# Deciding the gate in two halves, and ScalarE scaling the experts' hidden rows, in a decoder kernel

## What is computed

```python
xn = rmsnorm(xf, gate_norm_w, EPS)
gate_logits = bitlinear(xn, gate_in_norm_w, gate_w)
probs = softmax(gate_logits)
topw, topi = top_k(probs, 2)
# one expert:
pos = cumsum(keep0) - 1            # over the tokens in order
keep = keep0 & (pos < C)           # C = 512, the room of an expert
xin = xf[tok] where valid
h = bitlinear(xin, gpn, gpw)
g, y = split(h)
out = bitlinear(silu(g) * y, dpn, dpw)
outputs.at[tok].add(out * wtok)
# bitlinear(x, norm_w, w):
xn = rmsnorm(x, norm_w, 1e-8)
q = round(xn * 127 / max(|xn|)) per row;  weights rounded to -1, 0, 1 times their mean
```

## Time and profile before

| | us |
|---|---|
| median of three runs | 2256.37 |
| lowest, highest | 2253.13, 2257.48 |
| the profiled execution's own time | 2251.49 |
| its span in the trace | 2249.6 |

### The profile page before, as it was taken

One profiled execution on the slowest core, in us unless ns is written; L12 is line 12 of the kernel. 1 busy time (PEld: TensorE's weight loads), 2 busy tenths in 40 slices (PEclk: granted clock), 3 DMA queues, 4 the chain that ended last, 5 costly groups with the idle time before them and its releaser, 6 DMA issues. The chain is left out here.

```text
span 2249.6 us, 43362 instructions
## 1 busy us (share of the span) xinstructions
PE 1692.2 (75%) x13330; PEld 1072.2 (48%) x13330; DVE 1547.2 (69%) x3321; ACT 1448.7 (64%) x2313; POOL 757.3 (34%) x732
## 2 busy tenths in 40 slices
PE   3789899999989999898589886021454478998577
PEld 1455555555555555555367664021122246666323
DVE  6877777777777777776525657662677377876775
ACT  2888889798888989798144656452455344443845
POOL 0534545455454545455000000085000156554000
PEclk9999999999999999999778878555566689999799
DMA  6222222222222222222312110362111311321001
GB/s 189 53 52 65 60 58 65 51 66 54 65 53 61 57 60 57 56 61 48 107 38 75 66 48 1 134 217 69 68 37 38 112 38 38 38 30 26 1 10 66
DMA packets 173816, 139.94 MB, mean 62 GB/s; under 512 B 83794, under 2 KB 155399, under 8 KB 173366
## 3 DMA queue, kind: packets, MB, share of 16 engines
q1 hardware_dynamic: 166710, 122.78, 20.5%
q0 software_dynamic: 6912, 14.71, 3.3%
HBM read 61.92 MB, written 20.97 MB: 37 GB/s over the span
## 5 line engine op out<-in xcount | busy, mean ns | idle before, releaser
L577 ACT ACTIVATE a_p_hi<-ps,a_probs_up,a_s_scale 128x512 f16<-128x512 f32 x512 | 397.7, 777 | 57.6 <-ACTq L575 56.8
L689 DVE TENSOR_REDUCE a_top<-ps 128x2 f32<-128x1024 f32 x256 | 313.3, 1224 | 134.0 <-DVEq L688 133.9
L578 ACT ACTIVATE a_probs<-ps,a_probs_up,a_s_scale 128x512 f32<-128x512 f32 x512 | 398.4, 778 | 0.0
L917 POOL TENSOR_TENSOR a_p_lo<-a_probs,a_p_hi 128x1024 f16<-128x1024 f32 x128 | 278.4, 2175 | 208.9 <-POOLq L916 168.6
L905 POOL TENSOR_TENSOR a_ops<-a_ident_down,a_top 64x256 f16<-64x256 f32 x256 | 158.9, 621 | 344.7 <-POOLq L900 336.2
L698 DVE TENSOR_TENSOR a_p_lo<-a_probs,a_p_hi 128x1024 f16<-128x1024 f32 x128 | 182.6, 1427 | 41.1 <-DVEq L697 41.1
L441 PE MATMUL ps<-a_ops 128*128 128x512 f16 x512 | 196.3, 383 | 17.6 <-PEq L439 17.6
L460 PE MATMUL ps<-a_v_hi,a_p_hi 128*128 128x65 f16 x2048 | 206.2, 197 | 3.2 <-PEq L455 2.9
L463 PE MATMUL ps<-a_v_lo,a_p_hi 128*128 128x64 f16 x2048 | 206.1, 195 | 0.0
L464 PE MATMUL ps<-a_v_hi,a_p_lo 128*128 128x65 f16 x2048 | 206.0, 196 | 0.0
L460 PEld LDWEIGHTS ps<-a_v_hi,a_p_hi 128*128 128x128 f16 x2048 | 191.6, 99 | 23.9 <-issue 11.9
(11 more groups left out here) (495 smaller groups left out, 3723.4 us busy)
## 6 DMA issues: line engine op xcount, KB each, us to landing
a_ops<-a_qk SPq DMA_DIRECT2D x384, 128.0 KB, 2.3
f_w<-in_L_ffn_W_dram SPq DMA_DIRECT2D x16, 1024.0 KB, 7.5
a_qd<-a_qk SPq DMA_DIRECT2D x128, 64.0 KB, 2.2
g_stage<-in_L_attn_gp_w_dram SPq DMA_DIRECT2D x8, 1024.0 KB, 6.6
X<-in_x_dram SPq DMA_DIRECT2D x8, 512.0 KB, 9.6
expert_in<-g_w SPq DMA_DIRECT2D x8, 512.0 KB
g_stage<-in_L_attn_dp_w_dram SPq DMA_DIRECT2D x8, 512.0 KB, 7.6
e_x_in<-expert_in SPq DMA_DIRECT2D x8, 512.0 KB, 4.3
```

Of the source, the lines that this page charges most:

```text
L577: nc.scalar.activation(p_hi[:, h % 2, k, :], scores, ACT.Exp, bias=probs_up[:], scale=s_scale[:])
L578: nc.scalar.activation(probs[:, h % 2, k, :], scores, ACT.Exp, bias=probs_up[:], scale=s_scale[:]).then_inc(st_taken, 1)
L689: nc.vector.tensor_reduce(top[:, c % 2, 2 * pair:2 * pair + 2], ps[:, ROW:ROW + 2, :], AX.X, ALU.max).then_inc(row_taken, 1)
L917: nc.gpsimd.tensor_tensor(p_lo[:, h % 2, 2:KT, :], probs[:, h % 2, 2:KT, :], p_hi[:, h % 2, 2:KT, :], ALU.subtract).then_inc(p_made_pool, 1)
```

## The change

1. The gate's rows run in four stages rather than five (L1050 and the new methods): norms are folded into `gate_roots`, which makes the four inverse roots (one more reciprocal in place of a second chain) in one set of Newton rounds on 128x16. On ScalarE the squares move from `experts_rows` to their own `square`, between `quantise` and `pair_turned(b, 1)`. On TensorE `gates` moves from behind `f_rows` to behind the values. On VectorE `add_outputs` stands ahead of logits, roots and values.
2. The choice moves into `GateRows` and is made for tiles 0 to 15 and 16 to 31 apart, with a carry of counts between them. The first half stands in `middle`: the maximum in step 7, the choice at the start and the slots at the end of VectorE's step 8, the counts on TensorE in step 8; GpSimd sends the first 32 scatters as the last thing of its part of `middle`. The second half stands in the next block, ahead of the weights' staging. The zeros over the inbox are written in `middle`, from a tile (f_outT) that GpSimd clears.
3. In the experts VectorE weighs the rows by the norm weights alone as each tile comes (`weigh`) and takes maxima of these; the inverse root and the quantising factor are multiplied into one number by row (h_per). ScalarE scales by it and adds the rounding constant (`hidden_round`, four operations), then rounds as before. The weighed rows lie in gate_u, which is free by then. ScalarE rounds the next expert's rows ahead of the results.
4. In the masked attention `maximum` is split, and at t = 3 VectorE does `outputs` ahead of the maximum and of `add_x`.

Cut to its core:

```diff
-    NORMS, ROWS, SQUARES, QUANTISE, GATES = 1, 2, 3, 4, 5
+    VALUES, ROOTS, QUANTISE, GATES = 1, 2, 3, 4
+    CHOICE = B // gate.HALVES - 1 + GATES
...
+                gate.masks(pool)
+                nc.gpsimd.memset(outT[:].rearrange("p c s -> p (c s)"), 0.0).then_inc(zeros_made, 1)
...
+                pool.wait_ge(gate.zeroed, 16 * (E + 1))
+                pool.wait_ge(u_made, B // gate.HALVES)
+                gate.send(pool, 0)
...
-                    if 0 <= b - GATES < B:
-                        gates(b - GATES)
                     if b + 1 < B:
                         scores(b + 1, bank_of["scores", b + 1])
...
                         values(b, 1)
+                    if 0 <= b - GATES < B:
+                        gates(b - GATES)
                     if 1 <= b <= B:
                         for m in range(DC):
                             outputs(b - 1, m)
+                    if b == CHOICE + 1:
...
+                        gate.count(pe, bank_of["counts",])
...
+                    if b == CHOICE + 1:
+                        gate.choose(dve, 0)
+                    if b >= B and b - ROOTS < B:
+                        gate_roots(b - ROOTS)
                     if 1 <= b <= B:
                         add_outputs(b - 1)
...
+                    if b == CHOICE:
+                        gate.less_maximum(dve, 0)
...
+                    if b == CHOICE + 1:
+                        gate.slots(dve, 0, bank_of["counts",], free[bank_of["counts",]])
...
+                    gate.less_maximum(dve, HALF)
+                    gate.choose(dve, HALF)
+                    gate.slots(dve, HALF, 2)
...
+                    def hidden_round(j):
+                        act.wait_ge(h_factor, 1)
+                        act.sem_inc(h_factor, -1)
+                        for t in range(RT):
+                            nc.scalar.activation(weighed[:, j, t, :], weighed[:, j, t, :], ACT.Identity, scale=h_per[:, t:t + 1],
+                                                 bias=plus_round[:])
...
                         act.drain().then_inc(h_squared_all, 1)
+                        if not last:
+                            whole(r[:], a[:], a_round, r_made)
                         if not first:
                             results((j + 1) % 2)
...
+                    def weigh(e, j, tiles):
+
+                        dve.drain()
+                        for t in tiles:
+                            nc.vector.tensor_tensor(weighed[:, j, t, :], h[:, t, :], down_n[:, e, :], ALU.mult)
...
-                        for t in range(RT):
-                            nc.vector.scalar_tensor_tensor(out=h[:, j, t, :], in0=h[:, j, t, :], scalar=rstd[:, t:t + 1],
-                                                           in1=down_n[:, e, :], op0=ALU.mult, op1=ALU.mult)
+                        nc.vector.tensor_tensor(h_peak[:], h_peak[:], rstd[:], ALU.mult)
...
+                        if t == 3:
+                            outputs()
+                            if more:
+                                maximum(t)
+                            add_x(b, t - 1)
```

481 lines of the change are left out of this document (270 added, 211 removed).

## The result

| | before | changed |
|---|---|---|
| median, us | 2256.93 | 2228.86 |
| lowest, highest | 2253.13, 2261.93 | 2223.41, 2234.56 |
| profiled execution's own time | 2251.49 | 2223.41 |
| its span | 2249.6 | 2221.7 |

The ratio is 0.9875, with a 95% interval of 0.9842 to 0.9907: 28 us faster, where 22.5 was forecast (2228.9 against 2234). The sum came nearly right, but of its terms one was half of what it turned out to be and one had the wrong sign, and several pieces of the difference between the two traces stand in stretches that the change doesn't touch. Five kernels have a single execution each and are read from their traces alone: the experts' old order, the two with the gate product moved, and the two without the squares.

What follows compares the result with a forecast made beforehand. No engine is full; each touched stage is a ring of waits, bound by the one ending last. -12 (`middle` and gate stage) - 7.5 (experts) - 3 (masked attention) = -22.5, from the 2256.4 median to 2234 us; 80% range 2214 to 2250.

Steps and rivals of the forecast that it cites:

- The two edits that I priced: `middle`: squares leave the place ahead of the probabilities' copy (at most 5.1 us); gate's product behind the values (4.2 and 2.4).
- the product's wait ahead of step 5: `middle`, TensorE: no 3 us wait before the gate's product, step 5 near 31 us, as a sign in the later trace.
- 11.7 gross and 8 net: `middle`: TensorE waits removed, 11.7 us, less 3.6 for the squares' new place in four steps; net 8, bounds 0 and 13.
- rival A: Slower by the clock: `middle`'s steps 3 to 6 at step 5's pace, masked scores perhaps slow; 2273 us, chance 0.08.
- The first scatter: End of `middle`, GpSimd: first scatter starts at 1417.6, after VectorE's first slots at 1425.6 less part 1's 8 us.
- the block was held: `middle`'s end: 32 scatters at 1.28, 41 us, keep the block open to 1458.6; without them it would have ended near 1427.
- Rival B: `middle`'s end: scatters at the contended 1.65, 53 instead of 41 us, all behind 12 later; about 2245, chance 0.2.
- The order of the rounding: Experts, ScalarE: rounding the next rows ahead of the results takes 1.3 us from a period, from two TensorE waits.
- The scaling: Experts, ScalarE: four scalings of 0.75 add 3.0 us a period, while its idle of 2.58 goes.
- The mean of 22.8: Experts: mean period before, taken over seven experts against a forecast ring of 21.7, for -7.5, bounds 0 and -18.
- Rival C: Experts go to VectorE's ring, 19.4 us a period, 14 us more gain; 2220, chance 0.12.
- 0.4 us a batch: Masked attention: gain from taking the outputs earlier, counted for seven batches, -3 us in all, bounds +2 and -8.

Runs made afterwards that it cites:

- the experts' old order: Kernel before with part 3, but the next rows' rounding behind the results again on ScalarE; period mean 22.4 us over the first six.
- the best of these versions: Changed kernel with part 4 undone, 10 of the first 32 scatters left in `middle` and 22 behind the block's end; ratio 0.9796 (0.9768 to 0.9823).

## Why the prediction was right, point by point

**Part 1, `middle`.** Its steps 3 to 7 took 157.26 us before and 141.54 after, 15.7 less, and 8 were forecast with a bound of 13. The two edits that I priced are the two that the runs found (10.7 for the product's place; 3.9 for the squares in their old place, of which 2.4 remain in the new one), and the product's wait ahead of step 5 went as said. The step that failed is the price of a wait on TensorE. I added up idle time, 11.7 gross and 8 net, as if a wait that is taken away were gone and the work beside it stayed as long as it was. Neither held: over steps 3 to 6 TensorE's idle fell only from 20.3 to 16.3 us, since much of it moved to the next product, and its work fell from 110.2 to 98.0, at a higher clock. So 4 of the 16 us in these four steps are idle, and 12 are work that I had left as it was. My rival A was the same mechanism with the other sign, and it had a place in the range of possible losses but none in the gain.

**Part 2, the halves.** The mechanism was right link by link. The first scatter was forecast for 1417.6 and came at 1401.5. Counted from `middle`'s first weights that is 12.1 earlier: 3.6 stand ahead of step 2, where the change has no part that I know of, 7.7 are the larger gain in steps 3 to 7, and 0.9 stand behind step 7, though VectorE waited 2.98 us there for ScalarE's squares (up to 1381.89). The 32 took 41.0 us as forecast, the block was held until they were done, and 3.1 us lie between the last one's end and VectorE's next instruction, where I had 1.5. The second choice took 14.4 us instead of 15.8, the staging 76.0 instead of 77, the second scatters 57 instead of 53, hidden. The stage after `middle` ended 0.4 rather than 1.4 us behind the staging. For both stages together -12 was forecast; -26.1 was measured, -22.5 from step 2 on, and that is 10.5 more than forecast, 7.7 of it part 1's. The other 2.8 are small ones: the 0.9 ahead of the first scatter, 1.4 in the second choice, 1.0 in the staging and 1.0 behind it, less the 1.6 at the block's end. Rival B (contended scatters in `middle`) didn't come: all stood at 1.28, and VectorE had nothing but small work beside them. The contention that it described, scatters made slow by VectorE, stands beside the staging in both kernels (2.90 us for one). What came when the scatters were moved was the other way round: VectorE's slots were slow beside scatters of 0.97.

**Part 3, the experts.** -7.5 was forecast and -12.2 measured (13 alone). The scalings took 2.92 where 3.0 were taken, the wait ahead of them went, the period came to 21.0 instead of 21.7. Two terms were short. The order of the rounding was right in size (1.3 taken, 1.4 measured) though not in its split: the wait of 1.62 ahead of the next gate stayed at 1.61. The scaling I had as 0.4 longer a period (3.0 for the 2.58 of wait), and it measured 0.4 shorter. And the last period, 17.9 instead of 21.35, I had not looked at: 3.4 us in one place. The mean of 22.8 that I took for seven was that of the first six. Rival C, VectorE's ring at 19.4, didn't come: ScalarE had no wait left ahead of the scalings.

**Part 4, the masked attention.** -3 was forecast, with +2 as its bad end; alone it is +8.4. The wait went away as forecast and came back ahead of the turned normed rows. I had said that the batch ends with VectorE's root chain, which is right, and then still took 0.4 us a batch for a gain. The rows gave no ground for any: a batch is 31.1 with the edit at a clock of 1.00, and 31.1 without it at 0.94. And I had put the loss by the clock into rival A only, tied to `middle` (1.6 us a batch, 11 in all; 7.2 in these two traces), though the two have nothing to do with each other. So A should have been two rivals.

**The sum.** Forecast -22.5, measured -28.1 by the medians. By parts, from the traces: -22.5 from step 2 of `middle` to the experts' rows, -12.2 in the experts, +7.2 in the six masked batches, which makes -27.5. What is left of the two traces nearly cancels: -3.9 ahead of `middle`, -3.6 in it up to step 2, +1.0 ahead of the first masked batch and +6.2 from the last batch's normalising to the output. Whether that 6.2 belongs to part 4 isn't settled: this stretch took 170.8 to 172.0 us in the five traces with part 4 and 164.2 to 171.4 in the nine others. So the forecast owes its nearness to errors that cancel: parts 1 and 2 were 10.5 too small and part 3 4.7, and part 4 was 10 the other way. That the sum fell within 6 us is luck in part; the mechanism was right for the halves and for the experts.

## What to carry to other kernels

Where the granted clock in a stretch is below 1, a wait on TensorE that goes is not worth its length: the idle may only move (1.5 us less, where 6.6 had gone), and the work around it may get shorter (9.2 us) or longer with the clock. Price both, idle and work at either clock, for gains and losses alike. These runs don't tell beforehand which way the clock goes: without the squares, which is less work, two steps of the changed kernel took 6.3 and 4.1 us longer in its one execution. A program stage that ends with all engines charges every engine for the last one's tail: work that only one engine does late belongs behind that end, and the 13 us were there for the taking, though more than half of what the hold had cost came back as slower work beside the scatters. And a change of several parts is measured part by part: two calls in another order on ScalarE were worth 8 us, and one part had to be taken back out for the best of these versions, 2.0% under before.

## What the runs showed of the hardware

A stretch of the program that is nearly the same in all kernels (step 1 of `middle`) took either 24.1 or 31.9 to 32.1 us in fourteen traces, with nothing between, at granted clocks of 1.00 and 0.73. Where it was short, the stretch ahead of it was long (77.5 and 78.2 us from `middle`'s first transfer against 73.5 to 77.0 in the other twelve), so that a difference of 8 us in one step of two profiles was 3.6 over both. A step is to be compared with its neighbours.

One TensorE group moved, with the same instructions in the two steps, took 59.0 or 49.8 us of work at mean granted clocks of 0.77 and 0.80 or 0.84 and 0.94; the idle differed by 1.5.

VectorE's short operations, with waits of 0.4 to 1.1 us between them that the profile puts down to nothing, took 14.9 us for a chain that takes 5.2 alone, beside indirect scatters of 0.97 us, and in two other runs 8 and 20 us; in one of these the waits went on for 4 us without a scatter being issued. GpSimd's pace (1.28) stayed as it was. The Trainium skill ("SBUF — State Buffer", section "Who interferes with whom") has an exclusive lock between the two in which whoever issues first blocks the other, for VectorE's 2-port modes and, against a GpSimd instruction that reads SBUF, for operations with two SBUF inputs. These rows don't follow it: 9 us of the same kinds of operations, the choice from 1421.3 to 1430.5, ran beside the same scatters unheld, and waits stood where no scatter was issued. So the lock alone doesn't account for what was measured.
